# A perceiver block's transformer: two pieces of weight splitting and four tile normalisations moved in ScalarE's order

## The reference

```python
x = x + cross_attention(ctx_1024, _layernorm(x), mask)      # 16 heads, 4096 context rows per batch
x = x + causal_attention(_layernorm(x), Qw, Kw, Vw)          # one head of 256
x = x + transformer(_layernorm(x), wqkv, wo, w1, w2, ...)    # DEPTH = 2 layers
return x
```

```python
h = shift_token(x)                       # the right half of the features comes from the row above
q, k, v = split(h @ wqkv)                # 8 heads of 64
q, k = l2norm(q) * qs, l2norm(k) * ksc; q, k = rotary_xpos(q, k)
x = x + local_attention(q, k, v) @ wo    # windows of 128, each also sees the window before it
h = layernorm(shift_token(x)) * lg + lb
a, g = split(h @ w1 + b1)                # two halves of 682
x = x + (a * gelu(g)) @ w2 + b2
```

## Time and profile before

| | us |
|---|---|
| three runs, median (lowest to highest) | 1061.09 (1059.42 to 1062.51) |
| the profiled execution's own time | 1058.91 |
| its span, first to last instruction | 1057.1 |
| PE busy in the span | 1014.4 (96%) |
| DVE busy | 814.4 (77%) |
| ACT busy | 664.2 (63%) |
| POOL busy | 205.1 (19%) |

### The profile page before, as it was taken

One profiled execution on the slowest core, in us unless ns is written; L12 is line 12 of the kernel. 1 busy time (PEld: TensorE's weight loads), 2 busy tenths in 40 slices (PEclk: granted clock), 3 DMA queues, 4 the chain that ended last, 5 costly groups with the idle time before them and its releaser, 6 DMA issues. The chain is left out here.

```text
span 1057.1 us, 25664 instructions
## 1 busy us (share of the span) xinstructions
PE 1014.4 (96%) x8683; PEld 942.2 (89%) x8684; DVE 814.4 (77%) x3009; ACT 664.2 (63%) x1542; POOL 205.1 (19%) x265
## 2 busy tenths in 40 slices
PE   6999999999999999999999998988999999999997
PEld 5899999999999999999999998966878989889887
DVE  6887777695877786877786787589988889889753
ACT  4865665674655665566565556576676776767753
POOL 0111111110111111111111111360006203263213
PEclk9999999999999999999999999999999999999999
DMA  6000000000000000000000100510010000010000
GB/s 203 23 12 3 10 1 1 11 12 4 11 2 0 11 13 3 12 2 0 11 13 2 34 2 2 186 17 2 1 41 21 2 1 21 25 58 2 1 22 21
DMA packets 28804, 21.64 MB, mean 20 GB/s; under 512 B 12095, under 2 KB 26268, under 8 KB 28700
## 3 DMA queue, kind: packets, MB, share of 16 engines
q1 hardware_dynamic: 28529, 20.21, 6.5%
q10 hardware_dynamic: 170, 0.07, 0.0%
HBM read 19.17 MB, written 1.05 MB: 19 GB/s over the span
## 5 line engine op out<-in xcount | busy, mean ns | idle before, releaser
L302 PEld LDWEIGHTS pv_ps<-v,pt 128*128 128x128 f32 x1792 | 214.9, 192 | 9.5 <-issue 3.0
L302 PE MATMUL pv_ps<-v,pt 128*128 128x65 f32 x1792 | 215.2, 272 | 3.3 <-DVE o L817 1.9
L795 DVE CUSTOM_DVE_ANT_0 s_sb<-s_ps,pen,mstate 128x256 f32<-128x256 f32 (+1 forms) x512 | 199.9, 446 | 13.9 <-issue 11.0
L509 ACT ACTIVATE probs<-s_sb,mbias 128x256 f32<-128x256 f32 (+1 forms) x512 | 203.2, 470 | 0.0
L669 POOL TENSOR_TENSOR o<-o,alpha 128x260 f32<-128x260 f32 x128 | 85.9, 671 | 561.8 <-ACT alpha L503 561.8
L518 ACT ACTIVATE pt<-turn 128x512 f32<-128x512 f32 x128 | 76.3, 596 | 122.9 <-PE turn L289 109.0
L289 PE MATMUL turn<-ident,probs 128*128 128x128 f32 x896 | 123.8, 278 | 0.1
L289 PEld LDWEIGHTS turn<-ident,probs 128*128 128x128 f32 x896 | 98.8, 144 | 9.5 <-issue 0.3
L817 DVE TENSOR_TENSOR o<-o,pv_ps 128x260 f32<-128x260 f32 x128 | 54.0, 422 | 46.1 <-PE pv_ps L302 34.9
L278 PE MATMUL s_ps<-kh,qh 64*128 64x256 f32 (+1 forms) x512 | 78.8, 304 | 2.8 <-DVE x L839 1.5
L767 DVE TENSOR_TENSOR kl<-proj,kh 128x512 fp32r<-128x512 f32 (+1 forms) x63 | 41.3, 655 | 51.6 <-ACT kh L496 51.0
(11 more groups left out here) (431 smaller groups left out, 2732.0 us busy)
## 6 DMA issues: line engine op xcount, KB each, us to landing
raw<-in_ctx SPq DMA_DIRECT2D x24, 128.0 KB, 2.1
f_wqkv_raw<-in_L_ffn_wqkv SPq DMA_DIRECT2D x6, 512.0 KB, 5.2
f_w_raw<-in_L_ffn_w SPq DMA_DIRECT2D x8, 256.0 KB, 4.9
f_w_raw<-in_L_ffn_w SPq DMA_DIRECT2D x2, 640.0 KB
wkv_raw<-in_L_xattn_Wkv SPq DMA_DIRECT2D x1, 1024.0 KB, 6.8
wout_raw<-in_L_xattn_Wout SPq DMA_DIRECT2D x1, 1024.0 KB, 11.0
f_wo_raw<-in_L_ffn_wo SPq DMA_DIRECT2D x2, 512.0 KB, 4.5
x<-in_x SPq DMA_DIRECT2D x1, 768.0 KB, 8.7
```

The source lines that it names most:

```text
L302: last = pe.matmul(t.pv_ps[:, u, :], t.pt[g % 2][:, u, kt, :], t.v[:, kt, h, :], start=(kt == 0), stop=(kt == kts - 1))
L509: last = act.activation(t.probs[g % 2][:, u, 0:kts * P], t.s_sb[g % 2][:, u, 0:kts * P], ACT.Exp, bias=t.mbias[:, at:at + 1], scale=0.125)
L795: last = dve.tensor_tensor_reduce(out=t.s_sb[g % 2][:, u, 0:width], in0=t.s_ps[g % 2][:, u, 0:width], in1=t.pen[:, 0:width], scale=1.0, sc ...
```

## The change

Only ACT's stream changes. The two `high_piece` calls go from before the loop to T = 0, behind `heads_hi(0, 1, 1)`. The call of `first_normed` for tiles 4 to 7 goes from the end of T = 0 to T = 1, behind `exponentials(0, 2, 0)`.

```diff
             squares(0, 1)
             first_normed(3, range(QT, 2 * QT))
-            high_piece(act, s, ("w12", first["w12"]))
-            high_piece(act, s, ("w2", first["w2"]))
             for T in range(0, UNITS + 1):
...
                 if valid(T - 1):
                     exponentials(T - 1, 2, 0)
+                if T == 1:
+                    first_normed(5, range(2 * QT, TILES))
                 if valid(T - 2):
                     deviations(T - 2)
...
                 if valid(T):
                     heads_hi(T, 1, 1, t.g[2])
                 if T == 0:
+                    high_piece(act, s, ("w12", first["w12"]))
+                    high_piece(act, s, ("w2", first["w2"]))
                     first_deviations(4, slice(2 * QT, TILES))
...
                 if valid(T + 1):
                     squares(T + 1, 1)
-                if T == 0:
-                    first_normed(5, range(2 * QT, TILES))
```

## The result

| | before | changed |
|---|---|---|
| median of six runs each | 1060.80 us | 1055.31 us |
| lowest to highest | 1059.42 to 1062.51 | 1054.52 to 1057.13 |
| ratio, 95% interval | | 0.9945, 0.993 to 0.996 |
| all executions of this study whose clock was recorded | 74: median 1061.45, mean granted clock 0.990 | 17: median 1055.44, mean granted clock 0.994 |
| the profiled execution: time, span, clock | 1058.91, 1057.1, 0.995 | 1057.13, 1055.3, 0.992 |

The change makes the kernel faster by about 5.5 to 6 us, 0.55%. 3.2 us were forecast. One thing to see at once: the two profiled executions are only 1.8 us apart, the medians 5.5. The profile of before is from an execution faster than all of its six runs, that of the changed kernel from the slowest of its six. With a single profile on each side, the difference between the spans is not the effect of the change.

The account below looks back on a forecast made before the run. PE, busy 96% of the span, was taken to bind, with holes waiting on ACT and DVE. +4.0 (first edit) - 1.6 (POOL's lock) + 1.3 (DVE's idle) - 0.5 (clock) = 3.2 us, giving 1057.9 us; range 1055.3 to 1060.9.

Parts of the forecast that it names:

- The high parts: ACT's w12 and w2 pieces moved into its 2.49 us wait for DVE's first statistics: cost 0, about 0.3 us of wait left.
- `f_bias`: DVE's pair 0 bias, due at 718.4 us, held by POOL's long w2 subtraction: a stall of 1.9 us.
- the offset: DVE's `first_offsets` after pair 0's bias, held by POOL's last small piece: 0.45 us.
- `scores(0,0)`: On PE, starts 4.0 us earlier once ACT's high parts leave the front of the loop.
- DVE's reduction of `rotate_cos(1,0)`: On DVE, starts at 721.0 instead of 723.43 us: 2.4 us left after POOL's hold-up.
- Both new holes: New PE idle times of about 1.8 us each, before `scores(0,2)` and before `weighted_values(0,1)`.
- the clock's term in the sum: Half clock on PE after its new idle time before `weighted_values(0,1)` costs 1.1 us; half, 0.5 us, was subtracted.
- The second edit: Moving ACT's four normalisations to T = 1 lets DVE's idle times before `latents_lo(2)` vanish: 1.3 us gained.
- the second move buys nothing: Rival: DVE binds all of T = 1, so moving the normalisations gains nothing; 1.3 us gain in all, 1059.8 us; chance 0.11.
- the first edit's share: Moving ACT's high parts leaves DVE 2.4 us earlier at T = 1, after POOL's hold-up.
- The lock: Rival: POOL's w2 subtraction does not hold DVE's `f_bias`; gain 4.6 us, 1056.5 us; chance 0.12.
- The clock rival: Idle time before `scores(0,2)` puts PE's dense stretch at half clock, 1.6 us lost per dip; slower, to 1063.3 us; chance 0.07.

## Why the prediction was off by almost a factor of two

**What held.** Most steps on the chain came out close. The high parts cost nothing in their new place, and ACT's wait there shrank to 0.28 us. `f_bias` stalled 1.6 us (1.9 taken), and the offset 0.6 (0.45 taken) in two of three profiles and nothing in the third, and the stalled instruction ended with POOL's, as by the Trainium skill's rule of an exclusive lock (SBUF — State Buffer, the section on its two separate sides); the trace agrees, with 719.69 and 719.67 us, and the run with the low parts held back confirms that POOL's instruction is the cause, with 0.16 us. From `turn_heads(0,0,0)` on, `scores(0,0)` came 15.83 us later before and 11.55 now: 4.3 us, 4.0 taken. DVE's reduction of `rotate_cos(1,0)` came 2.8 us earlier (18.99 and 16.15 us; 2.4 taken). Both new holes lie where forecast, at 1.42 and 1.36 us instead of 1.8. At full clock the stretch fell from 37.26 us (before, holes filled) to 34.18 (changed) or 33.56 (changed, holes filled), 3.1 to 3.7; in the first profiles, with dips in both, by 2.3. And what was won by then reached the end: the first profile of before and the third of the changed kernel have no dip between 745 us and the last microseconds, and the stretch differs by 4.58 us (38.65 and 34.07), the whole from `turn_heads(0,0,0)` to the end by 4.6 (352.7 and 348.0).

**What failed: the clock's term in the sum.** I took half clock for something that the change might bring in ("- 0.5 (half of the clock's 1.1)"), against a kernel before that had what its one profile showed. That profile is the luckiest execution of it that I have by its clock. The median of the runs stood 2.2 us above it, and I carried that over as a constant offset. It is no constant, since it goes with the clock: the profiled execution had 0.995, the 74 others 0.990 on average. That difference of 0.005 over 1058 us is some 11 us more at half clock (0.005 x 1058 / 0.5). For the changed kernel the offset had the other sign: its profiled execution took 1057.13 us, 1.8 above the median, where I had forecast 1055.7.

Two comparisons split the gain of 5.5 to 6 us. Holes filled in both, it is 1058.72 less 1054.46, 4.3 us; the intervals of the two ratios would allow anything from 1 to 7. At the same granted clock of 0.992, 17 executions of before have a median of 1059.8 us and five of the changed kernel one of 1057.0: 2.7 us. With the stretch's 3.1 to 3.7 us, the chain's part is about 3 to 4 us, near the 3.7 that my sum has without its clock term. The rest, about 2 us, goes with the clock, whose mean rose from 0.990 to 0.994. Filling the holes wins 2.3 us in the kernel before, clear of the scatter, and 1.0 in the changed one, which is not. That fits with the change having closed the 2.84 us hole, and the 1.91 us one, itself: holes of 2.84 and 1.91 us gave way to holes of 1.42 and 1.36. So the sign of the term was wrong.

**The second edit** was priced wrongly as well. I gave it 1.3 us of DVE's idle time, and that idle time was the clock's: filling the hole removes it with neither edit in. On the chain the second edit is worth 0.2 (34.35 against 34.18 us), as in my rival "the second move buys nothing". What I took for the first edit's share, 2.4 us of DVE's, was then too little: at full clock the stretch is 37.26 us before and 34.35 with the first edit alone, 2.9. That the two together come near the chain's gain is in part luck. In the median the second edit's share is 1.2 us (1056.89 against 1055.67), which the overlapping intervals don't show to be more than nothing; with the hole full and the normalisations in the old place the time is 1054.05 us. So what it may win on top of 0.2 goes with the open hole, that is with the clock.

**The rivals.** The lock did bite. The clock rival named a mechanism that is at work and forecast the wrong direction: PE's holes of over a microsecond went down in all, from 2.84, 1.60 and 1.91 us to 1.01, 1.42 and 1.36.

**What stays open.** How the gain divides between chain and clock is known to about a microsecond only: the stretch is from one profile each, and dips at 38, 650, 765 and 935 us differ from profile to profile. The one at 935 us came in two of three profiles of the changed kernel and in neither of the two of before, and what follows comes some 0.9 us later with it. Why the clock falls behind a hole of 1.36 us in one execution and not in the next was not settled. The same holds for the 0.8 to 1.4 us of POOL's hold-ups in the stretch, which no whole execution showed. Moving the low parts' own work away from every DVE instruction with two SBUF operands was not tried.

## What to carry to other kernels

Before a sum is set against a profile, compare the profiled execution's granted clock with that of the other runs: where they differ, the sum lacks a term. Count PE's holes of over a microsecond as a cost of their own, beside what waits behind them. Closing them with products that nobody reads was worth about 2 us in the kernel before (ratio 0.9981), and nothing that could be told from the scatter in the changed one, whose longest holes were already shorter. And moving work off one engine moves what it triggers on another: ACT's high parts took POOL's subtractions along, and those stopped DVE in the new place.

## What the runs showed of the hardware

- The granted clock fell to half at the hole of 2.84 us in all four profiles that have it unfilled, from 0.5 us before the hole's end to 1.3 us behind it. At holes of 1.91 and 1.36 us it did in some executions and not in others, with the same instructions and the same holes; none of the profiles shows it at the hole of 1.42 us. One stretch of the same kernel took 34.18 and 36.32 us by it.
- An execution of this kernel and its variants had a mean granted clock from 0.984 to 0.998. In the kernel before, 0.986 went with 1064.7 us and 0.992 with 1059.8.
- A DVE instruction of 128x4 elements, 0.16 us by itself, took 1.77 us beside a POOL subtraction of 128x1280 and ended with it. The next one, also 128x4, took 0.75 us in some executions and 0.15 in others. Statistics over one operand, 0.4 us each, show no such hold-up beside POOL.
- Work that is moved away from where it holds an engine up can hold it up elsewhere: the kernel before with POOL's low parts held back had DVE 2.4 us ahead at 712 us, lost 1.3 us at another `f_bias` at 762, and was no faster (ratio 1.0008, 0.9991 to 1.0026) at a mean granted clock of 0.9875.
